# A decoder layer on one core: values in two transfers, later quotients, and Wo loaded and split by half blocks in fifteen batches in place of whole blocks in eight

## The reference, cut to what matters

```
x   = layernorm(x + mlp(x))              # 16 x 112 x 1024, gated MLP with a top-k mask
q   = x @ Wq                             # 32 heads of 32
k,v = ctx @ Wk, ctx @ Wv                 # ctx: 16 x 375 x 1024; 8 heads of 32, each serves 4 query heads
o   = softmax(q k^T / sqrt(32)) v
x   = layernorm(x + o @ Wo)              # Wo: 1024 x 1024
x   = layernorm(x + dequantised_linear(x))
```

## Time and profile before

| | |
|---|---|
| median of 3 runs | 2531.68 us |
| profiled execution, time / span | 2542.13 / 2540.3 us |
| PE busy | 2435.3 us (96%) |
| POOL, DVE, ACT busy | 1402.1, 1268.1, 1049.1 us |
| context pass, 0 to 310 us: PE busy | 301.15 of 310 |
| MLP and queries, 310 to 1855: PE busy | 1531.93 of 1545 |
| attention, 1855 to 2308.4: PE busy | 382.06 of 453.4 |
| finish, 2308.4 to 2540.3: PE busy | 220.12 of 231.9 |

### The profile page before, as it was taken

The page is one execution under the profiler, slowest core; times in us unless marked ns, Lnnn a source line. Parts: engine busy times, 40 slices in busy tenths (PEclk is TensorE's granted clock), DMA queues, the critical chain, the costliest instruction groups (busy, mean ns, idle before and its releaser), DMA issues. The chain is left out here.

```text
span 2540.3 us, 33218 instructions
## 1 busy us (share of the span) xinstructions
PE 2435.3 (96%) x12861; PEld 2126.1 (84%) x12874; DVE 1268.1 (50%) x1779; ACT 1049.1 (41%) x1531; POOL 1402.1 (55%) x626
## 2 busy tenths in 40 slices
PE   9999999999999999999999999999988888888998
PEld 9999999988999889999899998899866666656775
DVE  4762304861018820079400486254467777764665
ACT  2112235533337333363423553233266767681111
POOL 5344244865447755458554585454467887782221
PEclk9999999999999999999999999999998999998999
DMA  6565533333332343333333233589956765555772
GB/s 206 169 189 176 195 112 100 106 117 125 113 100 100 123 127 113 100 101 126 108 115 115 96 108 98 186 256 292 264 150 160 188 168 150 154 151 158 177 175 87
DMA packets 254447, 371.75 MB, mean 146 GB/s; under 512 B 126641, under 2 KB 178865, under 8 KB 254033
## 3 DMA queue, kind: packets, MB, share of 16 engines
q1 hardware_dynamic: 254288, 369.61, 49.0%
HBM read 290.15 MB, written 78.70 MB: 145 GB/s over the span
## 5 line engine op out<-in xcount | busy, mean ns | idle before, releaser
L995 POOL TENSOR_TENSOR gp_w_lo<-cy_raw,gp_w_hi 128x1024 fp32r<-128x1024 f32 (+2 forms) x299 | 721.0, 2413 | 611.8 <-ACT gp_w_hi L870 611.3
L183 PE MATMUL gp_acc<-gp_x_hi,gp_w_hi 128*128 128x448 f32 x1504 | 558.6, 371 | 2.6 <-ACT gp_row L921 2.5
L185 PE MATMUL gp_acc<-gp_x_hi,gp_w_lo 128*128 128x448 f32 x1504 | 550.2, 366 | 0.0
L184 PE MATMUL gp_acc<-gp_x_lo,gp_w_hi 128*128 128x448 f32 x1504 | 550.1, 366 | 0.0
L870 ACT CAST gp_w_hi<-cy_raw 128x1024 fp32r<-128x1024 f32 (+2 forms) x300 | 307.1, 1026 | 315.0 <-PE gp_acc L185 308.7
L1463 POOL TENSOR_TENSOR ap_e_lo<-ap_e,ap_e_hi 125x1344 fp32r<-125x1344 f32 x109 | 331.0, 3069 | 95.4 <-ACT ap_e_hi L1490 74.7
L183 PEld LDWEIGHTS gp_acc<-gp_x_hi,gp_w_hi 128*128 128x128 f32 x1504 | 283.2, 188 | 25.9 <-ACT gp_row L921 4.0
L185 PEld LDWEIGHTS gp_acc<-gp_x_hi,gp_w_lo 128*128 128x128 f32 x1504 | 282.9, 188 | 22.1
L184 PEld LDWEIGHTS gp_acc<-gp_x_lo,gp_w_hi 128*128 128x128 f32 x1504 | 283.3, 188 | 20.9
L481 DVE TENSOR_REDUCE gp_sel_unit<-gp_keys 112x4 f32<-112x2048 f32 x4 | 9.1, 2286 | 550.3 <-ACT gp_keys L882 550.3
L183 PE MATMUL gp_acc<-gp_h_hi,gp_w_hi 128*128 128x448 f32 (+1 forms) x704 | 267.9, 381 | 8.4 <-DVE gp_h_lo L1058 5.6
(11 more groups left out here) (207 smaller groups left out, 4355.1 us busy)
## 6 DMA issues: line engine op xcount, KB each, us to landing
cy_raw<-in_w_gu SPq DMA_DIRECT2D x172, 512.0 KB, 3.3
cy_raw<-in_w_d SPq DMA_DIRECT2D x80, 512.0 KB, 3.6
cp_c_raw<-in_ctx_t SPq DMA_DIRECT2D x32, 750.0 KB, 6.7
cy_raw<-in_w_q SPq DMA_DIRECT2D x32, 512.0 KB, 4.6
q_scratch<-gp_q_out SPq DMA_DIRECT2D x64, 224.0 KB, 6.2
cy_qs<-q_scratch SPq DMA_DIRECT2D x64, 224.0 KB, 4.1
k_scratch<-cp_k_out SPq DMA_DIRECT2D x32, 376.0 KB
cy_ks<-k_scratch SPq DMA_DIRECT2D x64, 188.0 KB, 4.8
```

The source lines that it names most:

```text
L183: nc.tensor.matmul(out, wh, xh, start=first, stop=False)
L184: nc.tensor.matmul(out, wh, xl, start=False, stop=False)
L185: return nc.tensor.matmul(out, wl, xh, start=False, stop=last)
L995: last = nc.gpsimd.tensor_tensor(o, i, hi.bitcast(F32), ALU.subtract)
```

## The change

`fetch_v` becomes a helper that issues two DMAs, rows 0 to 111 (S = 112) and rows 112 to 124, on the same semaphore; PE waits for 32 a batch in place of 16. The loads of all 16 batches go this way. Wo is handled in 16 half blocks of 128 x 512, numbered k (block k // 2, column half k mod 2): parts 0 and 1 in batch 0, part n + 1 in each of batches 1 to 14. The places in the lists (load at h = 3, ACT at step 20, POOL ahead of h = 6) stay. `quotients(0)` moves from step 14 to step 18 of batch 15, behind the rounding of group h = 5, and `quotients(1)` from step 17 to the end of DVE's list, behind the work on group h = 7.

```diff
+    def fetch_v(self, sp, vs, vd, n):
+        flat = vs[:].bitcast(F32).rearrange("p t v w -> p (t v w)")
+        for rows in (slice(0, S), slice(S, KN)):
+            sp.dma_start(flat[rows], vd[n, rows]).then_inc(self.v_loaded[n % 2], 16)
...
                 if p == 26:
-                    sp.dma_start(cy.vs0[:].bitcast(F32).rearrange("p t v w -> p (t v w)"), vd[0]).then_inc(cy.v_loaded[0], 16)
+                    cy.fetch_v(sp, cy.vs0, vd, 0)
...
-    QUOTIENTS_AT = (14, 17)
+    QUOTIENTS_AT = 18
...
+    def cols(k):
+        return slice(D // 2 * (k % 2), D // 2 * (k % 2 + 1))
+
+    def w_parts(n):
+        return (0, 1) if n == 0 else (n + 1,) if n < B - 1 else ()
...
-        wo_raw = [m.sb(f"wo_raw{i}", [P, D], F32) for i in range(2)]
+        wo_raw = [m.sb(f"wo_raw{i}", [P, D // 2], F32) for i in range(2)]
...
             def fetch_v(n):
                 if n >= 2:
                     sp.wait_ge(pv, KV * (n - 1))
-                sp.dma_start(vs[n % 2][:].bitcast(F32).rearrange("p t v w -> p (t v w)"),
-                             vd[n]).then_inc(v_loaded[n % 2], 16)
+                cy.fetch_v(sp, vs[n % 2], vd, n)
...
             def load_w(k):
                 if k >= 2:
                     sp.wait_ge(wo_lo_done, k - 1)
-                sp.dma_start(wo_raw[k % 2][:], w_o[:, k, :]).then_inc(wo_loaded[k % 2], 16)
+                sp.dma_start(wo_raw[k % 2][:], w_o[:, k // 2, cols(k)]).then_inc(wo_loaded[k % 2], 16)
...
-                    if h == W_LOAD_AT and n < KV:
-                        load_w(n)
+                    if h == W_LOAD_AT:
+                        for k in w_parts(n):
+                            load_w(k)
...
             def split_w(k):
                 pool.wait_ge(wo_hi_done, k + 1)
-                nc.gpsimd.tensor_tensor(wo_lo[:, k, :], wo_raw[k % 2][:], wo_hi[:, k, :].bitcast(F32),
+                nc.gpsimd.tensor_tensor(wo_lo[:, k // 2, cols(k)], wo_raw[k % 2][:], wo_hi[:, k // 2, cols(k)].bitcast(F32),
                                         ALU.subtract).then_inc(wo_lo_done, 1)
...
-                if g % KV == W_SPLIT_AT and g // KV < KV:
+                if g % KV == W_SPLIT_AT:
                     pool.wait_ge(lo_pool, lo_of_pool(g - 1))
-                    split_w(g // KV)
+                    for k in w_parts(g // KV):
+                        split_w(k)
...
-                nc.scalar.copy(wo_hi[:, k, :], wo_raw[k % 2][:]).then_inc(wo_hi_done, 1)
+                nc.scalar.copy(wo_hi[:, k // 2, cols(k)], wo_raw[k % 2][:]).then_inc(wo_hi_done, 1)
...
-                    if n == B - 1 and x in QUOTIENTS_AT:
-                        quotients(QUOTIENTS_AT.index(x))
+                    if n == B - 1 and x == QUOTIENTS_AT:
+                        quotients(0)
             follow(KV * B - 1)
+            quotients(1)
...
                     if h == 0:
-                        pe.wait_ge(v_loaded[n % 2], 16 * (n // 2 + 1))
+                        pe.wait_ge(cy.v_loaded[n % 2], 32 * (n // 2 + 1))
```

More of the change, by code:

```diff
@@ L1342, in attend_pass @@
                                                             cy.nm_put)
-        qk_loaded, v_loaded, o_put, recip, r_stored = cy.qk_loaded, cy.v_loaded, cy.o_put, cy.recip, cy.r_stored
+        qk_loaded, o_put, recip, r_stored = cy.qk_loaded, cy.o_put, cy.recip, cy.r_stored
         wo_loaded = [m.sem(f"wo_loaded{i}") for i in range(2)]
@@ L1513, in _ @@
                         take(g - LAG - 1)
-                    if x == KT * W_SPLIT_AT + 2 and n < KV:
-                        split_w(n)
+                    if x == KT * W_SPLIT_AT + 2:
+                        for k in w_parts(n):
+                            split_w(k)
                     if x == TURN_AT + 1 and n + 1 < B:
```

## The result

The changed kernel takes 2470.59 us, the median of 4 runs (2469.17 to 2470.96), where the kernel before took 2533.91 us in runs beside it (2531.49 to 2536.49). The ratio is 0.9749, 95% interval 0.9732 to 0.9766: 63.3 us less. 2471 was predicted, 60.6 us less. The profiled execution took 2470.96 us, its span 2468.8.

What follows compares the result with a forecast made beforehand. PE's waits in the attention, chiefly 33.3 us for values, and lost clock were taken as the bound; 51.6 us from the intervals plus 9 from the quotients, 60.6, off 2531.7 gave 2471 us, range 2456 to 2480.

Steps and rivals of the forecast that it cites:

- The values: Values in two transfers: landing 6.5 us after issue in place of 12.4, removing PE's 33.3 us of waits.
- Wo by halves: POOL's piece of Wo about 1.3 us; PE's wait for POOL shrinks from 1.87 us by 1.1.
- rival D: Values' landing unchanged, 125 rows already use all engines; half blocks only shift waits: 2520 to 2532 us, chance 0.08.
- The sum of the intervals: Attention's 14 intervals between turns: 315.0 plus waits 15.4 plus clock 6, together 336.4 us, 51.6 less than 388.0.
- Clock: Time lost to lowered PE clock in the 14 intervals: 6 us left of 19.9, bounds 0 and 19.9.
- The quotients: End of the attention, batch 15: PE's 7.55 us wait for DVE goes; 9 us gained, bounds 0 and 12.
- the next limit: End of the attention: ACT's copy, which waited 2.92 us for a store of denominators, is late next; PE resumes at 2293.3.
- DVE's tail becomes the end of the pass: End of the attention: the case in which moving the quotients gains 0 of the 9 us.
- Carrying the profile over: Whole kernel: 60.6 us subtracted in full from the 2531.7 median, though the profiled execution lay 10.4 us above it.
- A: POOL or DVE paces the batch, 24.1 to 24.8 us each: 2479 to 2488 us, chance 0.17.
- B: Values land only a little earlier, 10.2 us; PE still waits 1.3 to 2 us: 2502 us, chance 0.10.
- C: The two value transfers serialize, each paying its fixed time: 33 us slower, 2565 us, chance 0.04.

Runs made afterwards that it cites:

- The cut at 96: The changed kernel with the values cut at row 96 in place of 112, transfers of 96 and 29 rows: 2581.10 us, ratio 1.0170.
- the early issue: The kernel before, one transfer of 125 rows, its issue moved from h = 7 to h = 4 of SP's list: 2543.49 us, ratio 1.0013.

## Why the prediction was right

The steps in its own order.

- **The values.** Right in mechanism and size. The wait is closed in a loop that the prediction saw only in part: turn of the maxima, 5.2 us later SP's issue, 12.4 us later PE's start on the values, 9.45 us later the next turn, together the 27.0 us of that batch (1875.22, 1880.41, 1892.81, 1902.26). PE's 1.87 us for POOL lay beside the 12.4, so they were no gain of their own. The landing was estimated at 6.5 us and is 6.9 in the median; PE takes the values up 8.2 to 8.9 us after the issue (predicted 7.8 to 8.9). The cut at 96 gave 14.5 where 14 was expected, and in the early issue the small transfer behind the large one was held up. That five engines carry 125 rows was an inference; the five updates and the five packets in flight bear it out.
- The Trainium skill's rule on the number of engines (DMA: Bandwidth & Descriptors, "Why a DMA increments its semaphore by 16 and not by 1": the largest number up to 16 that divides the rows) agrees with all four cases, in time and in the count of updates: 125 rows (by it 5 engines) 11.7 us from issue to PE's start (mean), 96 + 29 (16 and 1) 14.5, 112 + 13 (16 and 13) and 120 + 5 (15 and 5) at most one wait for values of 0.5 us. The Trainium skill's other rule, not to cut a transfer in two because the parts serialize (same page, "Rules for kernel authors"), does not hold for these 125 rows: the measurement decides, 0.9799 for the cut alone.
- **Wo by halves.** The piece was 1.29 us, 1.3 predicted; PE's wait 0.77, 0.7 to 0.8 predicted; that whole blocks could not run at 22.5 held (24.7 to 25.7 us). Wrong was the list of bounds: by itself this part costs 11 us, and its lower bound was set at no loss (rival D: "half blocks only shift waits"). The shift is not neutral. In single batches of the kernel before, a batch less its waits takes 22.4 to 22.8 us in three cases with a wait for values of 0.5 to 1.3 us and in one of 2.8, and 23.8 to 25.4 in the ten others, nine of them with 1.9 to 4.2; so one long idle stretch for PE may lower the clock where two short ones did not. This was not isolated, and it has exceptions: with whole blocks and the values in time, six batches with a single wait of 1.8 to 1.9 us ran at clock 0.93. Why half blocks alone cost 11 us stays open.
- **The sum of the intervals.** Predicted 336.4, measured 332.5. Waits 15.4 predicted, 13.2 measured. Clock 6 predicted, and only the first interval (clock 0.93) shows any. A batch without waits takes 22.8 in place of 22.5.
- **The quotients.** Predicted 9, measured 7.7 alone and 6.2 within the change. The place given for the next limit (ACT's copy behind the store of denominators, PE 1.48 us) was right in part: PE did wait there for ACT's copy, but the copy came directly behind ACT's rounding of the first tile (1.04 us, begun when DVE's quotient was ready), not behind a store. And two terms were missed. POOL's subtraction for h = 6 was done 32.8 us behind the last turn and not 30.6, and PE waited 2.29 us for it; the last output was stored at 36.2, not at about 34. And the bound named as 0, "DVE's tail becomes the end of the pass", came partly true: the first operation of the second quotient takes 3.38 us in place of 1.21 while POOL works beside it, and so DVE's list ends at 2238.80, 1.25 us behind SP's last issue, with the barrier after it.
- **Carrying the profile over.** That 2471 was met to 0.4 us is luck. The sum of 60.6 us was near the 61.7 of intervals and tail because two misses nearly cancel: the intervals lost 3.9 us more than predicted and the tail 2.8 less. And it was carried over in full from a profiled execution that lay 10.4 us above the median; the profile after was to take 2481.5 us and took 2470.96, 0.4 above its median. The spans differ by 71.5 us, and the 9.8 beyond intervals and tail are spread before the first turn and in the finish pass.
- **Rivals.** A has a true core: POOL does pace the batch, at 23.6 and not 24.1 to 24.8, and by its order rather than its sum. B and C fell with the waits for values, and D with the five updates and five packets in flight as well.

## What to carry to other kernels

Look at the rows (slowest dimension) of every transfer whose landing is long for its size: 125 rows ran on 5 engines and 29 on one, and the 125 held up small transfers behind them. Issuing them earlier only moved the wait. When a large wait is removed, recompute the loop that comes next by order, not by busy sums: the same 1.3 us of work cost up to 0.7 us a batch at one place of POOL's list and nothing at another. An edit that only makes a wait ahead of a later, fixed arrival shorter gives nothing, and here it cost 0.4%, for a reason not shown. A forecast from one profile is no better than the spread of the executions, here 10 us in the 14 intervals of two kernels with the same code there.

## What the runs showed of the hardware that was not expected

- 125 rows of 6336 bytes moved with five packets in flight (median), 29 such rows with one: 12.0 and 14.5 us from issue to the last update, where 112 + 13 rows took 6.9.
- 14 KB issued 5 us behind the one transfer of 125 rows landed in 6.5 us (median; up to 7.5), and in 2.1 without it ahead.
- A DVE operation on 128 x 1024 floats took 1.21 us alone and 3.38 us beside POOL's subtraction of the same size, at the same place in three kernels (3.38 or 3.39). POOL's took 3.67 us then and 2.35 a little later, without DVE beside it.
- Once nothing but engines paced it, the batch repeated to within 0.07 us over 13 batches; with a DMA in the loop it varied from 24.8 to 30.5.
- The kernel before spread over 2528.3 to 2547.0 us over all its runs here, the changed one over 2469.2 to 2476.5 (54 and 9 runs).
